# Four stacked graph layers on one core: VectorE operations rewritten to read one SBUF tensor, work moved to GpSimd and ScalarE, steps split into halves

## What is computed

```python
# layer 0: hypergraph convolution; H = (adj != 0)
xw  = x @ W1.T ; Dn = 1/(H @ adj[0]) ; Be = 1/H.sum(nodes)
h   = relu(Dn * (H @ (Be * (H.T @ xw))) + b1)
y   = conv(layer_norm(h) * gamma + beta, W2) ; out = y + x
# layer 1: graph attention
e   = leaky_relu(Wh @ a1 + (Wh @ a2).T, 0.2); e = where(adj > 0.5, e, -9e15)
out = elu(softmax(e, axis=1) @ Wh)
# layer 2: diffusion
al  = adj * exp(leaky_relu(sj + si + ab, 0.2)); T = al / sum(al)
out = relu(sum_k (T^k X) @ Wk[k] + bk[k])
# layer 3: weights per node
w   = softmax(((q @ k.T) / 8 * adj).sum(-1), over nodes); out = w * v
```

## Time and profile before

| what | us |
|---|---|
| median of 3 runs | 1734.89 (1734.82 to 1735.82) |
| profiled execution, span | 1733.3 |
| length of a round in the loop (from q to q) | 51.52 |
| PE busy in the span | 1505.2 (87%) |
| DVE busy in the span | 1470.3 (85%) |
| POOL busy in the span | 987.4 (57%) |
| ACT busy in the span | 985.4 (57%) |

### The profile page before, as it was taken

How to read it: one execution, slowest core, us unless ns; L and a number is a source line. 1 busy time by engine, 2 the same in 40 slices (tenths; PEclk the granted TensorE clock), 3 DMA queues, 4 the chain that set the end, 5 groups by cost and what they waited for, 6 DMA issues and landing times.

```text
span 1733.3 us, 34480 instructions
## 1 busy us (share of the span) xinstructions
PE 1505.2 (87%) x9936; PEld 1328.5 (77%) x9936; DVE 1470.3 (85%) x3980; ACT 985.4 (57%) x2153; POOL 987.4 (57%) x818
## 2 busy tenths in 40 slices
PE   4789989888988889998889898988898888998974
PEld 3678878778877778878778887877887777887864
DVE  6778888988888988888988888888888898888863
ACT  3345666555666555566555566655566655556643
POOL 4546566556566555656555656655656655565532
PEclk9899999999999999999999999999999999999987
DMA  4000111010111010011111011101011101011000
GB/s 136 19 31 1 44 44 43 30 42 18 36 42 42 30 42 24 30 42 42 40 32 40 15 42 42 42 30 42 13 41 42 42 30 42 19 35 42 25 25 31
DMA packets 75362, 63.21 MB, mean 36 GB/s; under 512 B 2880, under 2 KB 70848, under 8 KB 75200
## 3 DMA queue, kind: packets, MB, share of 16 engines
q1 hardware_dynamic: 75328, 62.80, 11.0%
HBM read 37.62 MB, written 16.78 MB: 31 GB/s over the span
## 4 chain that ended last, share of the span: by engine, by line
DVE 49%; issue 17%; ACT 8%; PE 7%; POOL 6%; DVEq 1%; POOLq 0%; ACTq 0%
DVE h L989 8%; DVE pT L1141 7%; DVE stats L971 6%; POOL rs L784 3%; DVE mv L975 3%; PE ps L296 2%; DVE z L1110 2%; POOL p L794 2%; PE ps L311 2%; DVE x L1118 2%; DVE p L1078 2%; ACT yT_hi L650 2%; DVE hsq L1089 2%; DVE cnt L1001 2%; DVE q L1135 2%
## 5 line engine op out<-in xcount | busy, mean ns | idle before, releaser
L624 ACT ACTIVATE p<-ps,rs 128x256 f32<-128x256 f32 x384 | 154.4, 478 | 228.7 <-PE ps L315 200.0
L833 POOL TENSOR_TENSOR hT_lo<-hT,hT_hi 128x512 fp32r<-128x512 f32 x96 | 125.6, 1314 | 247.9 <-ACT hT_hi L641 236.9
L794 POOL TENSOR_TENSOR p<-p,bk 128x512 f32<-128x512 f32 x64 | 84.8, 1325 | 283.4 <-ACT p L624 283.2
L784 POOL TENSOR_TENSOR rs<-var_e,neg_half 128x4 f32<-128x4 f32 x160 | 188.3, 1177 | 23.7
L384 PE MATMUL ps<-ident,h 128*128 128x128 f32 x768 | 131.1, 287 | 55.0 <-DVE h L989 52.8
L311 PE MATMUL ps<-wl_hi,h2T_hi 128*128 128x256 f32 (+1 forms) x768 | 174.4, 309 | 1.4 <-DVE h2T_lo L893 1.4
L384 PEld LDWEIGHTS ps<-ident,h 128*128 128x128 f32 x768 | 84.5, 142 | 95.0 <-DVE h L989 93.0
L315 PE MATMUL ps<-wl_hi,h2T_lo 128*128 128x256 f32 (+1 forms) x768 | 156.0, 285 | 0.0
L311 PE MATMUL ps<-wl_lo,h2T_hi 128*128 128x256 f32 (+1 forms) x768 | 155.3, 284 | 0.0
L989 DVE TENSOR_SCALAR h<-x,mv 128x256 f32<-128x256 f32 x256 | 150.9, 610 | 2.3
L296 PE MATMUL ps<-p,alT 128*128 128x256 f32 (+1 forms) x512 | 127.6, 391 | 20.0 <-POOL alT L861 15.6
(11 more groups left out here) (168 smaller groups left out, 4573.5 us busy)
## 6 DMA issues: line engine op xcount, KB each, us to landing
x_in<-in_x SPq DMA_DIRECT2D x32, 512.0 KB, 4.3
out_x<-x SPq DMA_DIRECT2D x32, 512.0 KB, 2.8
adj_f<-in_adjT SPq DMA_DIRECT2D x32, 256.0 KB, 3.0
adj_m<-in_adjT SPq DMA_DIRECT2D x32, 256.0 KB, 2.7
adj_l<-adj_m SPq DMA_DIRECT2D x32, 256.0 KB, 2.3
hsq<-in_rows SPq DMA_DIRECT2D x1, 1152.5 KB, 8.9
vqk<-in_l_wk SPq DMA_DIRECT2D x3, 256.0 KB, 8.0
x<-in_w1T SPq DMA_DIRECT2D x1, 512.0 KB, 6.1
```

What stands on the lines that cost most here:

```text
L624: return act.activation(dst, src, ACT.Copy, scale=scale)
L784: pool.tensor_tensor(rs[:, layer, :], var_e[:, layer, :], neg_half[:], ALU.pow).then_inc(done, G)
L794: pool.tensor_tensor(p0[:, s, :], p0[:, s, :], bk[:].rearrange("p (a d) -> p a d", a=1) .broadcast_to((P, 2, D)), ALU.add).then_inc(S["p0b ...
L833: pool.tensor_tensor(hTs[1][:, hc, :], hT[:, hc, :], hTs[0][:, hc, :], ALU.subtract).then_inc(S["hT_lo"], 1 if hc else 2)
```

## The change

Every rewritten DVE operation now takes at most one tensor from SBUF, or writes an accumulator (`accum_out`) that nobody reads, into a new tile `unread`. The leaky ReLU of the attention (`front_leaky`) and the penalty (`next_penalty`) are not rewritten. In particular:

- `centred`: the maximum by 0 leaves the DVE operation, which gets an accumulator instead. ACT's copies of the transposes take `Relu` in place of `Copy`, and the low parts take the maximum (`low_of_relu`).
- The clamp of the counts (L1001) is gone; the count gets `EMPTY` added.
- `front_last_low` and `front_hs` leave DVE. POOL makes `hT_lo` for all four chunks (`front_lo`), and the sums (`add_h` twice, `join_h`).
- `mid_logits`: ACT computes both exponentials, exp(0.2 z + ...) into `zb` and exp(z + ...) in place in PSUM (8 operations per round of 128x128 where there were 4 and one of 128x512), and DVE takes their maximum (`mid_edges`).
- `elu`: DVE reads PSUM first, then ACT takes the exponential in place in PSUM, then DVE adds. ACT had gone first.
- `wh` is scaled by DVE out of PSUM (`front_values`), no longer by ACT. `front_norm` is gone.
- Two operations of the variance and one of the degrees go, one of `sjc` comes.
- POOL's operations on 128x1024 (`x4`, `xb`, `x3n`, `res0`) are split into halves, and `x4`, `rsqrt(0)` and `nmr` stand behind `alT` instead of ahead of it.
- `next_penalty` stands ahead of `front_inverse(0)`; `front_wh` waits for `deg_ready` where it waited for `deg_a`.

```diff
@@ centred (DVE)
-                    dve.tensor_scalar(dst[:, g, :], src[:, g, :], mv[:, layer, g, 0:1], 0.0, ALU.subtract,
-                                      ALU.max).then_inc(done, 1)
+                    dve.tensor_scalar(dst[:, g, :], src[:, g, :], mv[:, layer, g, 0:1], None, ALU.subtract, ALU.add,
+                                      accum_out=unread[:, layer, g:g + 1]).then_inc(done, 1)
@@ POOL
+            def add_h(r, k):
+                pool.wait_ge(S["hT_ready"], r.front(3 + k))
+                pool.tensor_tensor(hs[:, k, :], hT[:, k, :], hT[:, 2 + k, :], ALU.add).then_inc(S["hs_half"], G // 2)
+            def join_h(r):
+                pool.wait_ge(S["hs_half"], r.front(G))
+                pool.tensor_tensor(hs[:, 0, :], hs[:, 0, :], hs[:, 1, :], ALU.add).then_inc(S["hs_done"], G)
...
@@ ACT
+                for g in (2 * b, 2 * b + 1):
+                    act.activation(zb[:, g, :], ps[:, 4, g * C:(g + 1) * C], ACT.Exp, bias=sjc[:, 1, g:g + 1],
+                                   scale=SLOPE).then_inc(S["zb5_ready"], 1)
+                for g in (2 * b, 2 * b + 1):
+                    act.activation(ps[:, 4, g * C:(g + 1) * C], ps[:, 4, g * C:(g + 1) * C], ACT.Exp,
+                                   bias=sjc[:, 0, g:g + 1]).then_inc(S["eb_ready"], 1)
...
+            def keep_x3(r):
+                wait(act, S["x4_ready"], r.tail(G))
+                act.wait_ge(S["x3_ready"], r.late(G))
+                act.activation(x3[:], x3n[:], ACT.Copy).then_inc(S["x3_moved"], G)
...
@@ DVE
+                dve.tensor_tensor(zb[:], ps[:, 4, :].rearrange("p (g c) -> p g c", g=G), zb[:],
+                                  ALU.max).then_inc(S["zb_ready"], G)
...
-                dve.tensor_scalar(cnt[:, 1, :], cnt[:, 0, :], 1.0, None, ALU.max).then_inc(S["clamped"], G)
...
+            def front_values(r, b):
+                dve.wait_ge(S["rz_ready"], r.front(2 * b + 2))
+                for g in (2 * b, 2 * b + 1):
+                    dve.tensor_scalar(wh[:, g, :], ps[:, 4 + g, 0:D], rz[:, g:g + 1], rs[:, 1, g:g + 1], ALU.mult,
+                                      ALU.mult).then_inc(S["whs_ready"], 1)
```

More of the change, by code:

```diff
@@ L16 @@
 TINY = 1.2e-38
+EMPTY = 1e-30
 P = 128
@@ L371, in late_h3 @@
             def late_h3(r, b):
[L373 to L378, removed]
+                wait(pe, S["p1_copied"], r.mid(2 * b + 2))
+                if b == 0:
+                    wait(pe, S["hT_ready"], r.front(G))
@@ L400, in mid_p1, with mid_p2 @@
[L400 to L410, removed]
+            def mid_p2(r, g):
+                pe.wait_ge(S["h2T_copied"], r.mid(2 * (g // 2) + 2))
+                if g == 0:
+                    pe.wait_ge(S["h2T_lo"], r.mid(G))
+                else:
+                    wait(pe, S["hT_hi"], r.front(g))
+                split_product(ps[:, 4 + g, 0:D + 2], lambda a, c: h2Ts[a][:, g, c, :],
+                              lambda b, c: wl2s[b][:, c, K2:K2 + D + 2], KC,
+                              0, (S["h2T_lo"], r.mid(2 * (g // 2) + 2))).then_inc(S["p2_ready"], 1)
@@ new lines, in keep_x3, with norm_x @@
+            def keep_x3(r):
+                wait(act, S["x4_ready"], r.tail(G))
+                act.wait_ge(S["x3_ready"], r.late(G))
+                act.activation(x3[:], x3n[:], ACT.Copy).then_inc(S["x3_moved"], G)
+            def norm_x(r, b):
+                act.wait_ge(S["nmr_ready"], r.next(G))
+                wait(act, S["res0_ready"], r.front(G))
+                for g in (2 * b, 2 * b + 1):
+                    act.activation(h0[:, g, :], x_in[:, g, :], ACT.Relu, bias=nmr[:, 1, g:g + 1],
+                                   scale=rs[:, 0, g:g + 1]).then_inc(S["h0_ready"], 1)
@@ L706, in body @@
                     copy_h3T(r, 1)
-                    wait(act, S["x4_ready"], r.tail(G))
-                    act.activation(x3[:], x3n[:], ACT.Copy).then_inc(S["x3_moved"], G)
+                    keep_x3(r)
                 if r.has_next:
-                    act.wait_ge(S["nmr_ready"], r.next(G))
-                    wait(act, S["res0_ready"], r.front(G))
-                    for g in range(G):
-                        act.activation(h0[:, g, :], x_in[:, g, :], ACT.Relu, bias=nmr[:, 1, g:g + 1],
-                                       scale=rs[:, 0, g:g + 1]).then_inc(S["h0_ready"], 1)
+                    norm_x(r, 0)
+                    norm_x(r, 1)
                 if r.has_late:
@@ L829, in body @@
                 if r.has_front:
-                    for hc in range(HC - 1):
-                        pool.wait_ge(S["hT_hi"], r.front(hc + 1))
-                        pool.tensor_tensor(hTs[1][:, hc, :], hT[:, hc, :], hTs[0][:, hc, :],
-                                           ALU.subtract).then_inc(S["hT_lo"], 1 if hc else 2)
+                    front_lo(r, 0)
+                    front_lo(r, 1)
+                    front_lo(r, 2)
+                    front_lo(r, 3)
                 if r.has_mid:
```

698 lines of the change are left out of this document (392 added, 306 removed).

## The result

| | before | changed |
|---|---|---|
| median of the runs, us | 1735.36 (4 runs) | 1857.85 (1854.29 to 1860.38, 4 runs) |
| ratio | | 1.0704 (95%: 1.0689 to 1.0719) |
| profiled span, us | 1733.3 | 1858.5 |
| mean granted clock of PE, share of full speed | 0.982 | 0.916 |
| one round, q to q, us | 51.52 | 55.03 |

The account below looks back on a forecast made before the run. Bound: a ring of DVE, PE, POOL and ACT, with DVE operations held up by POOL. DVE loses 7.8 us a round, but the round falls only 51.5 to 50.5; about 30 rounds give 1705 us, range 1660 to 1755.

Parts of the forecast that it names:

- rival 1: Ring through POOL and ACT, about 17 handovers: longer than summed; at 0.25 us each, round 52.7 us, 1771 us; chance 0.27.
- What bounds the kernel: DVE, PE, POOL, ACT form one ring per round; some DVE forms wait for POOL's current operation, the new forms do not.
- the accumulators: DVE's 12 norm steps per round: 0.34 us each with accumulator, 6.2 us become 4.1, -2.1; bounds 0 to -3.
- the sum: DVE's terms per round: -7.8 us in all, leaving some 40 us, so DVE ceases to be the bound.
- The load: POOL rises from 30.6 to about 34 us a round, some 65% of the span; DVE some 72%.
- The wait at the sums: PE reaches `front_sums` at +23.5 us and waits 2.4 for POOL's last sum; they start at +25.9.
- the walk: Round the ring from `q`: 25.9 us to the sums, 24.5 from there to the next `q`, 50.4 in all.
- The leaky ReLUs, "4.2 us become about 1.2: -3": On DVE, per round: they get in at the seams between POOL's halves of `x3n` and `res`, gaining 3 us.
- My own lower bound of 0 gain: The leaky ReLU term on DVE was bounded from 0 to -3.3 us a round.
- The price of +0.5 for the penalty: On DVE, per round: the moved penalty, 0.42 us, now falls on a half of `res` and costs +0.5.
- The rest of the sum: Other DVE terms per round: `hT_lo` and sums to POOL -3.4 us, clamp -1.0, variance, degrees, `wcol` -0.4, `sjc` +0.25, `wh` +1.4.
- Rival 2: PE becomes the bound: only its own waits are left, about 48.3 us a round, 1639 us; chance 0.12.

Follow-up runs that it names:

- The filled wait: Changed kernel with 16 unread matmuls of 248 columns put on PE ahead of the sums of the hidden layer: 1748.24 us.
- half of it: Changed kernel with 8 unread matmuls in place of 16 in PE's wait at the sums: 1789.31 us.
- both taken away: Changed kernel with 16 unread matmuls in PE's wait at the sums and the leaky ReLUs ahead of `x3n`: 1698.78 us.
- the faster kernel: Changed kernel with the three sums back on DVE and the leaky ReLUs ahead of `x3n`: 1606.05 us; with `x4` moved earlier on POOL as well, 1605.82 us.

## Why the prediction was wrong

The direction was wrong: 1705 forecast, with a range of 1660 to 1755 and rival 1 at 1771 as the worst named, and 1858 measured.

- **What bounds the kernel, and the accumulators.** Right. The waits of DVE's norm steps for POOL are gone, and about 61 us a run hang on that, later effects included. The prediction priced them as 2.1 us a round of DVE's list; the run shows 2.5 us of PE's waits. From start to start the steps take 0.37 to 0.40 us, for the 0.34 of the sum.
- **The load.** Right for POOL in the round, 33.2 us for about 34 (its share is 58% for 65, since the round is longer). DVE's 71% for 72 is in part luck: it is busy for 40.7 us in the round, where the terms of the sum give 45.4 - 7.8 = 37.6 (the text there says some 40), and the round is longer as well.
- **The wait at the sums.** Right in place and size: 2.4 us forecast, 2.13 measured. **Wrong in price.** The step reads "PE reaches the sums at +23.5 and waits 2.4 us", and the walk then lets PE go on at the pace of the earlier trace rows. In this kernel the granted clock fell to half behind the wait, and PE took 3.2 us more in the round shown to reach the second `w2`. This cost was put at nothing without a reason. From the sums to the next `q` the walk had 24.5 us, measured were 27.7, while its points on POOL held: `alT` ended at +8.3 for +7.9 and `x4` at +12.96 for +13.0. PE started `wh` at +23.4 for +20.25; alone it would have been there at +19.7 by the walk, and 3.2 us of slow clock make that 22.9. The clock of the earlier trace rows stood at 1.00, and the prediction never asked whether it would stay when PE empties at a new place; the wait of 1.7 us that the kernel before has at full clock gave no warning. The filled wait shows it (110 us, the shorter leaky ReLU among them), and half of it shows that 1.24 us is enough in half of the rounds.
- **The leaky ReLUs, "4.2 us become about 1.2: -3".** Wrong: 3.0 stayed, and from `q` to the end of the values the round took 7.9 us, not 6.25; the sums came at +27.3 instead of +25.9. The rule was right (DVE gets in at a seam), the phase was not. The first ReLU arrived 1.26 us after `x3n` began, when the second half had just started; 0.3 us earlier, as in the rounds at full clock of the filled kernel, it takes 0.6. So its 0.9 us is a further price of the slow clock in this order of PE's work (with the sums later on PE it took 1.54 us in the rounds at full clock too). The second took 1.5 us with the slow clock and without, and that 1 us is an error of this term itself. My own lower bound of 0 gain was the better warning. The price of +0.5 for the penalty is tied to the same phase: it took 0.42 us here, since the late ReLUs had outlasted `res` (962.57).
- **The rest of the sum.** With both taken away the kernel runs in 1699 us, where the forecast was 1705. Part of that closeness is luck, since the ReLUs then take 0.42 each, less than the walk had.
- **Rival 1** named the ring and 17 handovers of 0.25 us. The handovers were not measured one by one, but the walk's points on POOL held to 0.5 us; what stretched the ring was PE's pace. `keep_x3` did wait for `x4`, as forecast, but ACT's next copy out of PSUM then waited 2.48 us for PE, and in the faster kernel too that wait was slack.
- **Rival 2** (only PE's own waits are left, 48.3 us a round) is about what the kernel with the sums on DVE and the ReLUs first does, at 47.3.

The Trainium skill bears on the missing step (TensorE: Matmul & The Clock Gate, HAM oscillation): it tells of a kernel whose matrix engine waits for a transfer at each tile and starts each tile at the lower clock. The trace agrees in kind, the granted clock at 1.00 up to the wait and 0.62 in the 9.03 us from the sums on; here the engine waited for POOL and not for a transfer, for 2.13 us.

## What to carry to other kernels

When work moves off a busy engine, walk the order up to the point where the matrix engine now waits, and price that wait twice: once for its length and once for the clock behind it, which in the round shown cost 3.2 us for a wait of 2.13. The second price can also be nothing, as behind the waits of 1.7 us before, so give both cases a chance. Work moved to an engine with a low busy share is not free if it lands in front of the operation that others wait for: three sums on POOL cost 194 us (clock and the ReLU's phase included), on DVE they lay in a hole. Where two engines exclude each other, do not forecast the phase in which they meet; order them with a wait, as the leaky ReLUs ahead of `x3n`, or price the whole of the other's operation.

## What the runs showed of the hardware that I had not expected

- Ahead of the one-column sums the granted clock fell behind a PE wait of 2.13 us in every round of the loop, behind 1.24 us in 15 of 27, and behind 0.36 us in every fourth (mean clock 0.916, 0.955 and 0.976).
- With the sixteen one-column matmuls in a row behind a wait of 0.29 us it fell in two rounds of three (0.961).
- Behind waits of 1.70 us (before) and 1.45 us (changed), both followed by matmuls of 128 columns, it stayed at 1.00. Two waits of 1.0 and 1.2 us close together, with matmuls of 256 columns, brought it down in every fourth round (0.965).
- POOL's sums of 128x512 take 1.25 us from start to start when DVE stays out of their way, as in the rows at 977.66 to 983.86 above.
